# Attention inside an eight-stage network on one core: three banks of scores, whole quads of products, stacks filled in 32-bit words

## What is computed

```python
# layer 0 (KV heads repeated twice)            # layer 1
scores = einsum('bsnd,btnd->bnst', q4, k4)*scale
probs  = softmax(scores, axis=-1)              # scores = where(tril, scores, -inf) before it
a_dot  = einsum('bnst,btnd->bsnd', probs, v4)
```

## Time and profile before

| | before |
|---|---|
| median of 3 runs | 4350.31 us (4349.63 to 4357.54) |
| profiled execution | 4356.75 us, its span 4354.7 us |
| TensorE busy | 3362.5 us, 77% of the span |
| VectorE busy | 2806.6 us, 64% |
| ScalarE busy | 1723.7 us, 40% |
| GpSimd busy | 1112.8 us, 26% |
| mean granted TensorE clock | 0.865 of full speed |
| first attention | about 168 to 645 us |
| causal attention | about 1436 to 1860 us |

### The profile page before, as it was taken

The page is one execution under the profiler, slowest core; times in us unless marked ns, Lnnn a source line. Parts: engine busy times, 40 slices in busy tenths (PEclk is TensorE's granted clock), DMA queues, the critical chain, the costliest instruction groups (busy, mean ns, idle before and its releaser), DMA issues. The chain is left out here.

```text
span 4354.7 us, 50885 instructions
## 1 busy us (share of the span) xinstructions
PE 3362.5 (77%) x13992; PEld 1542.8 (35%) x14109; DVE 2806.6 (64%) x4224; ACT 1723.7 (40%) x2599; POOL 1112.8 (26%) x942
## 2 busy tenths in 40 slices
PE   5598986999986598877897667566676668757998
PEld 3122225444443244443443222222222243533443
DVE  6887764333346576645333999999999953355444
ACT  2165661444435254534233455454545413212222
POOL 3211110000002221100000767677777710100000
PEclk7599996999988799969798788888887779878999
DMA  4411110000005423100001333333333310000000
GB/s 134 115 57 55 57 36 11 0 0 0 0 25 157 122 77 84 39 27 0 0 0 52 120 113 135 116 123 119 120 126 117 126 37 0 2 0 0 0 0 19
DMA packets 130940, 252.92 MB, mean 58 GB/s; under 512 B 24717, under 2 KB 100898, under 8 KB 113378
## 3 DMA queue, kind: packets, MB, share of 16 engines
q1 hardware_dynamic: 126674, 249.17, 17.4%
q0 software_dynamic: 4096, 1.59, 0.2%
HBM read 191.98 MB, written 56.89 MB: 57 GB/s over the span
## 5 line engine op out<-in xcount | busy, mean ns | idle before, releaser
L1855 POOL TENSOR_TENSOR a_g<-a_g,a_spread 128x1024 f32<-128x1024 f32 x256 | 659.1, 2581 | 587.6 <-DVE a_g L1813 587.6
L1615 PE MATMUL a_y<-a_g,ident 128*128 128x512 f32 x768 | 461.3, 740 | 368.1 <-POOL a_g L1860 218.6
L930 DVE TENSOR_REDUCE a_top<-a_sc 128x1 f32<-128x512 f32 (+3 forms) x1024 | 583.9, 590 | 210.0 <-PE a_sc L803 121.0
L886 ACT ACTIVATE a_prob<-a_st 128x1024 f32<-128x1024 f32 (+2 forms) x512 | 441.9, 864 | 410.0 <-PE a_st L820 248.6
L1813 DVE TENSOR_TENSOR_SCAN a_g<-a_decay,a_drive 128x512 f32<-128x512 f32 x512 | 595.4, 1201 | 3.9 <-DVE a_drive L1803 3.9
L455 DVE TENSOR_TENSOR f_s<-f_a,f_spread 128x512 f32<-128x512 f32 x392 | 268.1, 687 | 435.8 <-ACT f_a L440 268.8
L1735 ACT ACTIVATE a_decay<-a_delta,a_capped_a 128x512 f32<-128x512 f32 x512 | 337.1, 712 | 435.2 <-DVE a_capped_a L1785 235.4
L800 PE MATMUL a_sc<-a_k,a_q 96*128 96x512 bf16 (+3 forms) x1024 | 364.5, 362 | 89.5 <-POOL a_mask_k L740 32.5
L422 PE MATMUL f_y<-f_s,f_w 128*128 128x512 f32 x784 | 401.3, 599 | 20.9 <-DVE f_s L455 20.3
L415 PE MATMUL f_hid<-h,f_w 128*128 x784 | 406.3, 603 | 6.0 <-PEq L246 6.0
L1615 PEld LDWEIGHTS a_y<-a_g,ident 128*128 128x128 f32 x768 | 164.7, 229 | 636.9 <-issue 404.5
(11 more groups left out here) (327 smaller groups left out, 4830.9 us busy)
## 6 DMA issues: line engine op xcount, KB each, us to landing
a_spread<-a_bc_rows SPq DMA_DIRECT2D x128, 1024.0 KB, 4.7
a_q<-a_q_rows SPq DMA_DIRECT2D x64, 288.0 KB
a_pv_rows<-a_pv_sb SPq DMA_DIRECT2D x64, 256.0 KB, 2.2
a_q_rows<-p_qp SPq DMA_DIRECT2D x72, 128.0 KB
a_q_rows<-a1q_qp SPq DMA_DIRECT2D x72, 128.0 KB
a_k_rows<-a1q_kp SPq DMA_DIRECT2D x72, 128.0 KB
a_k<-a_k_rows SPq DMA_DIRECT2D x32, 288.0 KB
a_k_rows<-p_kp SPq DMA_DIRECT2D x72, 64.0 KB
```

Of the source, the lines that this page charges most:

```text
L886: nc.scalar.activation(prob[w % 2][:, j, 0:width(kp)], st[:, j % 2, 0:width(kp)], ACT.Exp, scale=a.scale).then_inc(s.exp_done, 1)
L930: nc.vector.tensor_reduce(top[:, t, n:n + 1], sc[:, t % 2, 0:w], AX.X, ALU.max).then_inc(s.maxed, 1)
L1615: last = nc.tensor.matmul(y[:, k, :], S.ident[:, :], g[:, n % 8, k, :], start=(n == 0), stop=False)
L1855: nc.gpsimd.tensor_tensor(g[:, n % 8, :, :], g[:, n % 8, :, :], spread[:, pair % 4, 2 + n % 2:3 + n % 2, :].to_broadcast([P, H2, L]), ALU. ...
```

## The change

Three banks of `sc` in place of two. `slot` numbers a chunk's tiles and turns in one sequence of 68 (a turn after tiles 4, 20, 36 and 52), and each takes bank slot % 3. A slot waits for the reduction or the copy of the slot three before it.

One bank of `pv` in place of two. `PIECES` is gone: a quad is multiplied for one block of keys at a time, over all its columns, at the end of rounds 1 and 3, behind both score tiles and behind `turn`.

The fills of `q0` and `k0` are done through a float32 view (`TWO_ONES` is the float32 whose two halves are bf16 ones), those of `k1` by two DMAs on SP from rows of `k0`. The masks are built behind the first of the four fills of `q0`.

```diff
+TWO_ONES = 1.0019378662109375
...
-    S.setup_primes += [(s.maxed, 2), (s.exp_done, 2), (s.pv_done, 2), (s.evacuated, 2)]
+    S.setup_primes += [(s.maxed, 3), (s.exp_done, 2), (s.pv_done, 2), (s.evacuated, 2)]
...
-        sc = ps("sc", [P, 2, L])
-        pv = ps("pv", [P, 2, L])
+        sc = ps("sc", [P, 3, L])
+        pv = ps("pv", [P, L])
...
-        if a.causal:
-            PIECES = [[(0, 0, 2 * P), (0, 2 * P, 2 * P), (1, 0, P + P // 2), (1, P + P // 2, P + P // 2)],
-                      [(0, 0, P), (0, P, P), (1, 0, P)]]
-        else:
-            PIECES = [[(0, 0, 2 * P), (0, 2 * P, 2 * P), (1, 0, 2 * P), (1, 2 * P, 2 * P)]] * 2
+        def slot(i):
+            return i + sum(1 for h in range(4) if i >= 16 * h + 4)
+        def turn_slot(h):
+            return 17 * h + 4
+        TILE_AT = {slot(i): i for i in range(64)}
...
             for r in (ROWS, ROWS + 28):
                 sp.dma_start(q[1][r:r + 28, :, :], q[0][P - 28:P, :, :]).then_inc(s.zeroed, 16)
-            sp.wait_ge(s.zeroed, 32 * call + 32)
+                sp.dma_start(kk[1][r:r + 28, :, :], kk[0][P - 28:P, :, :]).then_inc(s.zeroed, 16)
+            sp.wait_ge(s.zeroed, 64 * call + 64)
...
-                nc.gpsimd.memset(q[0][:, 4 * g:4 * g + 4, :], 0.0).then_inc(s.q_ready, 1)
+                nc.gpsimd.memset(q[0][:, 4 * g:4 * g + 4, :].bitcast(F32), 0.0).then_inc(s.q_ready, 1)
+                if a.causal and g == 0:
+                    nc.gpsimd.memset(mask_q[:, :], 0.0).then_inc(s.step, 1)
...
+            def bank_free(b, at, k):
+                p = at - 3 if at != 2 else -4
+                if p < 0:
+                    pe.wait_ge(s.maxed, (nB + b) * 64 + TILE_AT[p + 69] - 64 + 1 + 3)
+                elif p in TILE_AT:
+                    pe.wait_ge(s.maxed, (nB + b) * 64 + TILE_AT[p] + 1 + 3)
+                elif not (isinstance(b, int) and b == 0 and call == 0 and p == turn_slot(0)):
+                    pe.wait_ge(s.max_copied, 4 * (nB + b) + p // 17)
...
-                    if kp == 0:
-                        pe.wait_ge(s.evacuated, (nB + bb) * 4 + g + 1)
+                    if kp == 0:
+                        pe.wait_ge(s.evacuated, (nB + bb) * 4 + g + 2)
...
                         if A:
                             score_tile(b, 2 * w + j // 2, 2 * j % 4, k)
-                        if w == BEHIND:
-                            if B:
-                                products(b - 1, 7, k ^ 1, j)
-                        elif bb is not None:
-                            products(bb, wb - 1, kb, j)
-                        if A:
                             score_tile(b, 2 * w + j // 2, 2 * j % 4 + 1, k)
                         if j == 1 and w % 2 == 0:
-                            if w > 0 and A:
-                                turn(b, w // 2 - 1, (nB + b) * 64 + 8 * w + 2 + 1 + 2)
+                            h = w // 2
+                            reduced = (nB + b) * 64 + (16 * h + 1 + 1 if A else 0) + 3
+                            if h > 0 and A:
+                                turn(b, h - 1, turn_slot(h), reduced)
...
+                        if j % 2 == 1:
+                            if w == BEHIND:
+                                if B:
+                                    products(b - 1, 7, k ^ 1, j // 2)
+                            elif bb is not None:
+                                products(bb, wb - 1, kb, j // 2)
...
-            for k in range(2):
-                for g in range(4):
-                    n = KVH // 4
-                    nc.vector.memset(kk[k][64:P, n * g:n * g + n, :], 1.0).then_inc(s.k_ready, 1)
+            for g in range(4):
+                n = KVH // 4
+                nc.vector.memset(kk[0][64:P, n * g:n * g + n, :].bitcast(F32), TWO_ONES).then_inc(s.k_ready, 1)
```

More of the change, by code:

```diff
@@ L562, in attention_semaphores @@
     s, sem = State(), S.sem
-    s.calls = 0
+    s.calls, s.causal = 0, 0
     s.stack = [[sem(f"at_stack{k}{g}") for g in range(4)] for k in range(2)]
@@ L569, in attention_semaphores @@
     s.zeroed = sem("at_zeroed")
+    s.ones = sem("at_ones")
     s.v_ready = sem("at_v_ready")
@@ L786, in _ @@
             if a.causal:
-                pe.wait_ge(s.step, 2 * call + 6)
+                pe.wait_ge(s.step, 4 * s.causal + 4)
+            def bank_free(b, at, k):
[6 more added lines that the diff above has]
+                    pe.wait_ge(s.max_copied, 4 * (nB + b) + p // 17)
             def score_tile(b, n, t, k):
-                pe.wait_ge(s.maxed, (nB + b) * 64 + 4 * n + t + 1)
-                if t == 0 and n % 4 == 1 and not (isinstance(b, int) and b == 0 and call == 0 and n < 4):
-                    pe.wait_ge(s.max_copied, 4 * (nB + b) + n // 4)
+                at = slot(4 * n + t)
+                bank_free(b, at, k)
                 if n % 4 == 0 and t == 0:
@@ L822, in scores_of_keys, with products, turn @@
                 last.then_inc(s.st_done, 1)
-            def products(bb, w, k, piece):
+            def products(bb, w, k, kt):
                 g, kp = w // 2, w % 2
-                pieces = PIECES[kp]
-                if piece >= len(pieces):
-                    return
-                kt, off, wide = pieces[piece]
-                if piece == 0:
+                if kt == 0:
                     pe.wait_ge(s.exp_done, (nB + bb) * 32 + 4 * w + 4 + 2)
                     if kp == 0:
-                        pe.wait_ge(s.evacuated, (nB + bb) * 4 + g + 1)
+                        pe.wait_ge(s.evacuated, (nB + bb) * 4 + g + 2)
                     if w == 0:
                         pe.wait_ge(s.v_ready, nB + bb + 1)
-                col, first = SPAN[kp][kt][0] + off, SPAN[kp][kt][1] + off
+                col, first, wide = SPAN[kp][kt]
                 for j in range(4):
-                    last = nc.tensor.matmul(pv[32 * j:32 * j + 32, g % 2, first:first + wide],
+                    last = nc.tensor.matmul(pv[32 * j:32 * j + 32, first:L],
                                                 v[k][:, 2 * kp + kt, (4 * g + j) // HK, :],
-                                                prob[w % 2][:, j, col:col + wide], start=(kp == 0 and piece == 0),
+                                                prob[w % 2][:, j, col:col + wide], start=(kp == 0 and kt == 0),
                                                 stop=(kp == 1 and kt == 1), tile_position=(0, 32 * j),
                                                 skip_group_check=True)
-                if piece == len(pieces) - 1:
+                if kt == 1:
                     last.then_inc(s.pv_done, 1)
-            def turn(b, g, reduced):
+            def turn(b, g, at, reduced):
                 pe.wait_ge(s.max_parts, 4 * (nB + b) + g + 1)
@@ L938, in _ @@
             steps(dve, body)
+    if a.causal:
+        s.causal += 1
 def split3(chain, eng, src, rest, parts, between=lambda: None):
```

37 lines of the change are left out of this document (18 added, 19 removed).

## The result

The change is faster: 4246.82 us (median of 4 runs, 4243.23 to 4251.83) against 4352.00 us of the kernel before on the same chip (4 runs), a ratio of 0.9757, interval 0.9740 to 0.9774. The profiled execution has a span of 4244.7 us where the one before had 4354.7: 110.0 us less.

What follows compares the result with a forecast made beforehand. TensorE was taken to set the pace, VectorE near, with GpSimd's chain late next. Terms 22 + 39 + 13 = 74 us, against a median of 4350.3, gave 4276 us; own range 4246 to 4304, widened to 4240 to 4315.

Steps and rivals of the forecast that it cites:

- a chain of GpSimd that hides: Rival: GpSimd's split of the maxima before the turn does not bind; groups 11.9 and 9.6 us, time 4234, chance 0.10.
- groups, first attention, 29 intervals: Steady groups of the unmasked attention: period falls from 13.5 to 12.75 us, 29 x 0.75 = 22 us.
- groups, causal attention, 29 intervals: Steady groups of the causal attention: period falls from 11.5 to 10.15 us, 29 x 1.35 = 39 us.
- starts: Filling the stacks at both attentions' starts: 2.5 us saved in the first, 10 causal; together 13, bounds 5 and 18.
- A quad of 512 columns costs 1.00 us: TensorE's products: 512 columns take 0.15 + 4 x 0.21 = 1.00 us to the next instruction's start.
- The third bank removes the 0.68 us behind the copy of the turned rows: After each turn: its own slot among three banks frees the next score tile from VectorE's copy, saving 0.68 us.
- The turn waits for GpSimd: Before each turn: reductions and GpSimd's chain take 4.0 us against TensorE's 3.1, so it waits 0.9; period 12.75 us.
- One bank of products costs nothing here: First quad of a group: ScalarE's copy, about 0.65 us, fits inside two rounds of 1.76 us, or 1.32 causal; cost nothing.
- the rival of the clock: TensorE's waits and cycling through three banks lower its clock; a dozen groups at 1.2 GHz give 4396; chance 0.03.
- A switch there and back: TensorE going to and from the narrow product matmuls: 0.25 us; three fewer save 0.75 us per causal group.
- the last rival: Given back elsewhere: the loop's pauses or the maxima's DMA grow by what the groups gain; 4350; chance 0.02.
- the lower bound of 5: Least gain from the starts: only the causal reductions' 5.3 us comes through, the maxima's DMAs queueing behind the added ones.

Runs made afterwards that it cites:

- d_turn_late: The changed kernel with the turn issued behind the products of its round instead of ahead: 4219.24 us, ratio 0.9689 to the kernel before.
- j_one_bank: The kernel before with one bank of products in place of two, pieces and all else kept: 4373.87 us, ratio 1.0046.
- i_pieces: The changed kernel with products cut into the old pieces at their old places; three score banks, one product bank, new start kept: 4314.22 us, ratio 0.9903.
- c_halves: The changed kernel with each quad of the first attention cut into two halves back to back: 4263.56 us, ratio 0.9791 to the kernel before.
- h_before_unrolled: The kernel before with TensorE's loop over pairs of chunks written out, nothing else changed: 4328.36 us, ratio 0.9939.
- a_quads: The kernel before with whole quads of products between a round's two score tiles, two banks each and old fills kept: 4355.79 us, ratio 1.0000.
- b_fills: The kernel before with only the new start (32-bit fills, k1 by DMA, masks ahead): 4341.81 us, ratio 0.9969.
- f_v_first: The changed kernel with SyncE's first load of v issued ahead of the stacks of the last three groups: 4247.53 us, ratio 0.9749 to the kernel before.

## Why the prediction was right, and where it was not

The time of 4246.8 lies inside the range of 4240 to 4315, 29 us under the forecast of 4276, and the sign is as forecast. It lies 7 us above the range's lower end. That end was set for a chain of GpSimd that hides, and for other fills; what brought the time there was something else, 18 us of jumps and 12 of code outside the attentions, which the sum had at nothing. The terms that the text did size come to 79 where it had 74. By its own terms, for the profiled executions:

| term | forecast | trace |
|---|---|---|
| groups, first attention, 29 intervals | 22 | 28.7 (29 x 0.99) |
| groups, causal attention, 29 intervals | 39 | 43.5 (29 x 1.5) |
| starts | 13 | 6.9 (first fill to first turn copy: 22.7 to 19.8 and 29.8 to 25.8) |
| jumps of TensorE's loop | 0 | 18.1 (14.5 and 3.6) |
| first intervals and tails of the attentions | 0 | 1.1 |
| code ahead of, between and behind the attentions | 0 | 11.8 |
| sum | 74 | 110.1 |

**Steps that held.** A quad of 512 columns costs 1.00 us. The third bank removes the 0.68 us behind the copy of the turned rows. The turn waits for GpSimd: this was the step that set 12.75, and d_turn_late, which takes that wait away, reached the bound of the text for the first attention, 11.9, with 11.91. For the causal one, 9.6, only its shortest periods do; their mean is 9.88. One bank of products costs nothing here, for the reason given (ScalarE's copy lies inside two rounds); j_one_bank and i_pieces show that with pieces it would have cost 0.5 to 0.7 us a causal group. The clock stayed at 1.00 in both stretches, so the rival of the clock did not come, and the trace of the changed kernel does not bear out the rule that the prediction held against it (the Trainium skill, TensorE: Matmul & The Clock Gate, A second HAM failure mode) either.

**Sizes that were off.** The reductions lie 0.60 us apart when four are ready, not 0.65; over the chain's three gaps that is 0.15 us of the 0.22 by which the group is shorter than 12.75. TensorE waits 0.57 us for the turn instead of 0.9, and about 0.3 instead of 0.6 in the causal attention (4.2 us in 13 turns). A switch there and back is nearer 0.21 us than the 0.25 of the sum: between i_pieces and d_turn_late, in both of which the first attention's TensorE does not wait, four switches make 12.77 - 11.91 = 0.86. The estimate from the Trainium skill (TensorE: Matmul & The Clock Gate, Single matmul latency), 0.35, is further off.

**The step that failed.** The sum left the pauses at TensorE's loop as they were, and only the last rival named them, as something that could grow. The text counted what a quad saves in columns and switches, and not what it saves in instructions: four matmuls of 512 columns in place of eight of 256 take the loop's pass from 1820 TensorE records to 1306, and its jump back from about 5 us to 0.2. The jump in turn brought the lower clock behind it, so the two took 14.5 us. c_halves (the records back, the work the same: 17 us more) and h_before_unrolled (no jump: 27.9 us less) settle that. In the causal attention the pass fell from 2204 to 1822 and the jump still costs 5.5. The Trainium skill (Runtime: NRT & Kernel Launch, Instruction fetch mechanics) says that a taken branch whose target is not in the fetched window has to wait for a DMA fetch of it. The trace agrees that long jumps go with fetches. It does not bear out the figures given there (a window of two pages of 256 instructions each, room for 2048 instructions on TensorE) as the limit of a loop: a pass of 1306 records jumps back in 0.2 us, and one of 1814 does not. The view of the DMA queues, 205 to 585 us, shows the fetches (packets, MB, share of the span of the 16 engines), before and after:

```profile
q8 instruction: 28, 0.46, 0.5%
```

```profile
q8 instruction: 8, 0.13, 0.2%
```

In the same window a_quads has 9 packets and c_halves 30. h_before_unrolled has 23 and not one pause, so no pause goes with a fetch where the code runs straight on.

**The term that was too large.** The causal start: the reductions did come 10 us earlier, but the sum took the start to end there. Behind them stood GpSimd's copy of v, waiting for a load (14.2 us), and the maxima's two transfers (6.3 and 7.3 us); the text had put their delay only into the lower bound of 5, and 6.9 is near that bound. The added transfers were put at nothing too. Yet the causal attention's first two periods take 27.5 us, 7.5 more than two steady ones, where they took 26.0 before, 2.9 more; in b_fills, the new start alone, they take 32.0. What delays them was not tried by itself.

**Open.** 11.8 us lie in code that the change does not touch, 10.5 of them behind the causal attention. About 5 of the 110 us come of the pick of the execution: the profiled one of before lies 4.8 us above its median, that of the changed kernel at its own. Some of the 11.8 is real: b_fills measured 10.5 us by its medians with 3.4 in the starts, and all eight profiles with the new start are shorter behind the attention than all four with the old one. Through what the start reaches that code is open.

## What to carry to other kernels

When a wait moves ahead of a block of work in an engine's order, cost it against the chain that releases it: here the products could have stood in front of the turn and hidden it, 28 us more. Parts that look additive may be worth something only together: whole quads alone made the groups 0.25 and 0.4 us longer, the third bank alone gave 0.75 and 0.5 us a group, and both together 1.0 and 1.5. Count instructions per pass of a loop as well as microseconds, and look at the branch of the loop's line in the profile.

## What the runs showed of the hardware that was not expected

- TensorE's jump back of a loop took 0.2 us with 1306 to 1312 TensorE records in the pass (first attention of the changed kernel, a_quads, d_turn_late and f_v_first), and 3.4 to 6.4 us with 1814 to 2220 in every kernel that had such a pass. Written out, the code of the kernel before ran without pauses in their place.
- After such a jump (5.5 us at 391.6 us of the kernel before) TensorE's granted clock fell: 0.76 over 14.4 us, where it is 1.00 behind the short jump of the changed kernel. Jump and lower clock together made the period 7.3 us longer.
- A row-maximum reduction of 128 x 512 takes 0.68 us by itself; two in the kernel before took 1.34, four in the changed one 2.48, and four in a_quads 2.54. So they start 0.60 to 0.65 us apart when the next is ready.
- A TensorE that waits about 0.6 us in every 12.5 kept its clock here: the row of the first window shows 1.00.
